# Gated attention on one core: weights and context turned by the host, centring on VectorE and GpSimd, scores in column halves, and a new order of work

## What is computed

```
ln_out = _ln(_layernorm(x), ln_w, ln_b)
q  = _ln(fp8_linear(ln_out, wq))      # 16 heads of 128, 2 heads in each of 8 groups
k  = _ln(fp8_linear(ln_out, wk))      # 8 groups of 128
v  = fp8_linear(ln_out, wv)
qx = _ln(fp8_linear(ln_out, wqx))
kx, vx = split(cond @ w_kv_x.T)       # cond is ctx_2048; kx is normalised too
core = softmax(q k / sqrt(128)) v     # inside each batch of 64 tokens
xout = softmax(qx kx / sqrt(128)) vx
catq = fp8(clip(concat(core, xout) / proj_smooth))
x = x + tanh(g_xattn[0]) * (catq @ wproj.T) * scale
```

## Time and profile before

| | us |
|---|---|
| median of 3 runs | 1088.43 (1088.19 to 1090.18) |
| the profiled execution | 1089.46 |
| its span, first to last instruction | 1087.70 |
| opening, to the first projection | 35.47 |
| steps 0 and 1 | 49.33 |
| steps 2 to 13 | 324.22 (27.02 each) |
| step 14 | 26.37 |
| step 15 and the tail, to the last matmul at L315 | 61.48 |
| all that follows | 590.83 |

### The profile page before, as it was taken

One profiled execution on the slowest core, in us unless ns is written; L12 is line 12 of the kernel. 1 busy time (PEld: TensorE's weight loads), 2 busy tenths in 40 slices (PEclk: granted clock), 3 DMA queues, 4 the chain that ended last, 5 costly groups with the idle time before them and its releaser, 6 DMA issues. The chain is left out here.

```text
span 1087.7 us, 19039 instructions
## 1 busy us (share of the span) xinstructions
PE 981.8 (90%) x6752; PEld 822.5 (76%) x6752; DVE 749.8 (69%) x1301; ACT 539.2 (50%) x1655; POOL 268.0 (25%) x416
## 2 busy tenths in 40 slices
PE   3689999999999999956899999995999999699998
PEld 3579999999999998855677777773666665577776
DVE  8858878777878787776544454445688888666653
ACT  5566666666666665622433333323455554233332
POOL 2133333333333333302422222202010111323130
PEclk8799999999999999976799999997899998799999
DMA  5001020101010100004111111001000000110001
GB/s 180 1 2 59 2 59 2 59 2 59 2 60 1 60 4 18 2 1 176 44 47 47 47 46 46 3 0 59 1 1 0 0 0 2 58 59 30 29 0 39
DMA packets 22823, 35.40 MB, mean 33 GB/s; under 512 B 2016, under 2 KB 19552, under 8 KB 21600
## 3 DMA queue, kind: packets, MB, share of 16 engines
q1 hardware_dynamic: 22464, 34.38, 9.6%
q10 hardware_dynamic: 288, 0.10, 0.0%
HBM read 33.42 MB, written 1.05 MB: 32 GB/s over the span
## 5 line engine op out<-in xcount | busy, mean ns | idle before, releaser
L251 PE MATMUL ps<-wt_hi,xq 128*128 128x256 f32 (+1 forms) x512 | 124.7, 278 | 13.0 <-issue 10.3
L251 PE MATMUL ps<-wt_lo,xq 128*128 128x256 f32 (+1 forms) x512 | 122.2, 281 | 0.0
L458 ACT ACTIVATE square<-ps 128x128 bf16<-128x128 f32 x384 | 100.6, 293 | 39.7 <-PE ps L251 39.6
L251 PEld LDWEIGHTS ps<-wt_hi,xq 128*128 128x128 f32 x512 | 98.4, 192 | 17.2 <-issue 15.3
L1624 ACT ACTIVATE ca_probs<-ps 128x512 f32<-128x512 f32 x128 | 69.5, 595 | 82.8 <-PE ps L1544 82.8
L251 PEld LDWEIGHTS ps<-wt_lo,xq 128*128 128x128 f32 x512 | 98.9, 193 | 0.0
L1684 DVE TENSOR_REDUCE context_mx<-ps 128x4 f32<-128x1024 f32 x64 | 76.9, 1201 | 26.4 <-PE ps L1516 26.4
L596 POOL TENSOR_TENSOR rstd<-rstd,half_neg 128x6 f32<-128x6 f32 x64 | 87.2, 1362 | 5.0
L1210 POOL TENSOR_TENSOR moe_w_lo<-moe_w_all,moe_w_hi 128x384 fp32r<-128x384 f32 x48 | 54.8, 1176 | 135.4 <-ACT moe_w_hi L1311 135.4
L458 ACT ACTIVATION_READ_ACCUMULATOR square<-ps 128x1 f32 x384 | 86.0, 225 | 0.0
L1375 DVE TENSOR_TENSOR moe_act_g<-moe_act_g,ps 128x512 f32<-128x512 f32 x48 | 33.0, 687 | 70.5 <-PE ps L1246 70.5
(11 more groups left out here) (225 smaller groups left out, 2685.8 us busy)
## 6 DMA issues: line engine op xcount, KB each, us to landing
moe_w_all<-in_experts SPq DMA_DIRECT2D x8, 1152.0 KB, 5.4
wp_rows<-in_wproj SPq DMA_DIRECT2D x16, 256.0 KB, 2.9
ffn_codes<-in_codes SPq DMA_DIRECT2D x8, 384.0 KB, 3.2
ffn_w_scales<-in_code_scales SPq DMA_DIRECT2D x8, 384.0 KB, 3.9
w_rows<-in_wq SPq DMA_DIRECT2D x8, 256.0 KB, 3.7
w_rows<-in_wqx SPq DMA_DIRECT2D x8, 256.0 KB, 3.9
w_rows<-in_w_kv_x SPq DMA_DIRECT2D x16, 128.0 KB, 3.6
x_rows<-in_x SPq DMA_DIRECT2D x2, 512.0 KB, 5.1
```

The lines of the kernel that those rows point to most:

```text
L251: last = mm(ps[:, first + bank, col:col + n], left[:, c, tokens], w[:, c, wcol:wcol + n], start=(j == 0), stop=(j == len(steps) - 1))
L458: last = nc.scalar.activation(square[:, j, :], ps[:, bank, (j % 4) * P:(j % 4) * P + P], ACT.Square, scale=float(HD) ** -0.5, accum_out=su ...
```

## The change

- The host hands the weights over turned and grouped (`in_wt`, one load of 1 MB a group), the output weights as well (`in_wp`), and the context turned (`in_ctxT`). All matmuls and transposes on weights and context are gone from PE's part, and `centre` with them.
- Centring: DVE sums each of the six blocks over its 128 columns (`sum_weights`, one reduction of 128 x 768 for each of two chunks), POOL divides the sum and subtracts it in place, with the input scale (`centre_weights`, seven `tensor_scalar` of 128 x 128 and a tiny one for a chunk). ACT copies a chunk as the high part (128 x 1024), DVE subtracts for the low part (128 x 1024). The output weights are one ACT copy and one DVE subtraction of 128 x 1024 a group.
- Each score matmul is cut in two, one a head: 64 stationary columns, 64 moving ones, and output partitions 0 to 63 or 64 to 127.
- `take` is on ACT for both attentions. The values have three buffers instead of two, the squares two instead of one.
- All 16 steps are written out, with two more for what is left over, and their order is new: PE projects two tiles, works on scores and values, projects two more, and a unit's softmax now reaches from step `h + 1` into step `h + 2`.
- The opening has two roundings of the inputs in place of three; the third and the fourth stand in DVE's step 0. Ahead of the first input scaling ACT now has the high parts of the first weights, which wait for POOL's centring.

Core of the diff:

```diff
-            for j in range(4):
-                turn_weights(0, j, 4 + j)
...
+            def centre_weights(g, c):
+                pool.wait_ge(s["wt_summed"], CH * g + c + 1)
+                nc.gpsimd.tensor_scalar(w_mean[:, c, :], w_mean[:, c, :], 1.0 / HD, None, ALU.mult).then_inc(s["wt_mean"], 1)
...
+                for blk, scale in enumerate((0, 0, 2, 2, 4, None, None, 6)):
...
+                        last = nc.gpsimd.tensor_scalar(cols, cols, mean, factor, ALU.subtract, ALU.mult)
...
+            def sum_weights(g, c):
...
+                nc.vector.tensor_reduce(w_mean[:, c, :], w_in[:, c, 0:CENTRED * P].rearrange("p (b d) -> p b d", b=CENTRED),
+                                        AX.X, ALU.add).then_inc(s["wt_summed"], 1)
...
+            def weights_low(g, c):
+
+                dve.wait_ge(s["wt_hi_done"], CH * g + c + 1)
+                nc.vector.tensor_tensor(wt_lo[:, g % 2, c, :], w_in[:, c, :], wt_hi[:, g % 2, c, :].bitcast(F32), ALU.subtract
+                                        ).then_inc(s["wt_lo_done"], 1)
...
-                    last = mm(ps[:, S_BANK, b * SEQ:b * SEQ + SEQ], qT[:, r, batch].rearrange("p h s -> p (h s)"),
-                              kT[:, r, batch * SEQ:batch * SEQ + SEQ], start=True, stop=True)
+                    for head in range(HPG):
+                        last = mm(ps[SEQ * head:SEQ * head + SEQ, S_BANK, b * SEQ:b * SEQ + SEQ], qT[:, r, batch, head, :],
+                                  kT[:, r, batch * SEQ:batch * SEQ + SEQ], start=True, stop=True)
...
+                if i == 0 and h < 2:
+
+                    pe.wait_ge(s["quantised"], CH * h + CH)
...
+            for c in range(CH):
+                nc.scalar.copy(ctx_hi[:, c, :], ctx_in[:, c, :]).then_inc(s["c_high"], 1)
+            for c in range(CH):
+                weights_high(0, c)
...
+                if h == 0:
+
+                    quantise_rows(2)
+                if ahead and h % 2 == 0:
+                    sum_weights(g + 1, 0)
+                if ahead and h % 2 == 0:
+                    sum_weights(g + 1, 1)
+                if is_unit(h - 2):
+                    quantise(h - 2, 1)
```

609 lines of the change are left out of this document (253 added, 356 removed).

## The result

The changed kernel takes **1097.49 us** (median of 4 runs, 1096.78 to 1097.61). The kernel before took 1088.31 beside it; the ratio is 1.007, with a 95% interval of 1.0051 to 1.0089. The forecast was 1061, with a range of 1044 to 1083. The sign was wrong.

| stage | before | forecast | after |
|---|---|---|---|
| opening, to the first projection | 35.47 | 40.1 | 47.45 |
| steps 0 and 1 | 49.33 | 58.3 | 63.29 |
| steps 2 to 14 | 350.59 | 311.4 | 331.37 |
| step 15 and the tail | 61.48 | 59.5 | 62.41 |
| all that follows | 590.83 | 590.8 | 590.98 |

What follows compares the result with a forecast made beforehand. PE was taken to bound steps 2 to 13 at 27.02 us each. Opening +4.7, steps 0 and 1 +9.0, steps 2 to 14 -39.2 and tail -2.0 summed to -27.5, giving 1061 us, range 1044 to 1083.

Steps and rivals of the forecast that it cites:

- I take 0.3: POOL's centring operation of 128 x 128: 0.3 us between bounds of 0.13 and 0.39, 2.4 a chunk.
- The rival built on this price: POOL's centring on the path at 1.0 us an operation: +32 us, 1093, chance 0.07.
- PE bounds it.: Kernel before, steps 2 to 13: PE busy 316.56 of 324.22 us, so PE bounds the step of 27.02.
- The new step, walked: Timeline from the second projection's end: tile 0 normalised at 1.9, an odd step 23.2 us long.
- A step with POOL never in the way: Better rival, POOL never delaying a tile: 22.9 us a step, 1047 in all, chance 0.17.
- The shared wait: Even steps, DVE and POOL blocking each other during centring: 1.3 us late, bounds 0 and 2.5, step 24.5.
- Opening +4.7: Before the first projection: sums, centring and copies ahead of input scaling, PE starting at 40.1; bounds 0 and +9.
- Steps 0 and 1 +9.0: Third and fourth roundings in DVE's step 0 make PE wait: 58.3 us instead of 49.33.
- Halves at 1.15: Each score cut in halves takes 1.15 us instead of 1.70, saving 1.1 a step.
- PE's loss of 2.2 and 1.1 a step: PE's work per step falls 2.2 us by dropped weight turning and 1.1 by halved scores, to 23.7.
- Tail, -2.0: Step 15 and the tail: 59.5 us instead of 61.48, last projection ending at 16.2.
- Scores at 3.4: Rival with score halves not overlapping, 3.4 us a score: a step of 27.3, 1104 in all, chance 0.03.

Runs made afterwards that it cites:

- e1: The changed kernel with POOL's seven centring operations a chunk left out, sums and waits kept: 1066.8 us.
- e4: The changed kernel with POOL subtracting broadcast means in two 128 x 384 operations a chunk, factors put into ACT's and DVE's copies: 1079.3 us.
- e3: The kernel before with only its scores cut in halves: 1089.7 us, ratio 1.001.
- e16: The changed kernel with ACT's high copy of output weights moved ahead of the keys of tiles 2 and 3 in odd steps: 1093.7 us.
- e12: The changed kernel with POOL's chunk 0 behind the roots of tiles 2 and 3 (even step), chunk 1 behind those of tiles 0 and 1 (odd): 1087.1 us.
- e5: The changed kernel with input scalings ahead of ACT's high weight copies, both roundings ahead of DVE's low copies, third rounding before step 0: 1086.2 us.
- e9: A price list, not a version: POOL's centring replaced by groups of four operations a chunk of one form each; no kernel time given.

## Why the prediction was wrong, step by step

- **"I take 0.3" for POOL's operation of 128 x 128.** This is the first term that failed, and the dearest. It measured 0.78 alone and 0.94 on average. The bounds were rows of other forms: a cast by the column, and a two-tensor operation by a third. The price list shows that neither the form nor the fixed part carries over. The rival built on this price ("at 1.0 us", 1093, chance 0.07) described what came: the opening at +14.5 (measured +12.0), steps 0 and 1 at +13.9 (+14.0), 2.9 behind tile 2 in an even step (2.4). e1 puts the whole centring at 30.7 us, and e4, with a chunk as cheap as forecast, has the forecast's opening and steps 0 and 1 to 0.1. That rival deserved far more, since no row bounded the operation from above.
- **"PE bounds it."** Wrong as far as e3 tells: 1.1 a step less for PE brought nothing. The check with step 14 had pointed that way (2.7 less work, 0.8 less time), and the prediction took it for a remark on the order instead of on the bound.
- **The new step, walked: "tile 0 is ready at 1.9".** It was 3.5 in the step shown. The take on ACT ended where the walk had it (190.36, 3.0 ahead of the end of the second projection). But the rounding took 4.1 for 3.3, and the root 2.34 for 1.36, as the two hold each other up. This is the second step that failed. The lock was known and was booked for the centring only, not for the pair that meets in every step; e16 prices it at 0.96 in an odd step. That tile 0 comes 0.6 later behind an odd step was walked and is right: moving the copy of the output weights took 0.57 off an even step's wait (e16). A step with POOL never in the way had been put at 22.9; in e1 it is 24.2, and 24.4 on average.
- **"The shared wait", +1.3 in even steps.** The sum of the even step, 24.5, was too small by 2.1: the queue behind POOL cost 2.4 where 1.3 was booked (e12), and the other 1.0 is the wait for tile 0. Where the centring is in nobody's way in the queue, the lock costs 0.5 (e12, odd steps).
- **Opening +4.7**: +12.0. The mechanism was right (two chunks ahead of the scaling), its price was that of POOL. **Steps 0 and 1 +9.0**: +14.0, with the rounding in step 0 behind tile 3, as walked; the fourth rounding ended at 83.7, and step 1 started at 83.80 instead of 73.9. Another place for the roundings (e5) or for POOL's chunks (e12) takes 4.6 or 4.9 of it away.
- **Halves at 1.15**: right, 1.08. Their gain of 1.1 a step was not: with what PE waits for, 0.03 to 0.32 in the changed kernel and 0.54 without the centring. **PE's loss of 2.2 and 1.1 a step**: right; step 14 has 24.22 less a wait of 1.82, 22.4 of PE's work.
- **Tail, -2.0**: +0.9. The last projection of step 15 ended 17.1 behind its start instead of 16.2, by the same wait for tile 0, and the rest took 45.3 instead of 43.3.
- **Loads free, the rest untouched** (590.98 for 590.83): right.
- **The working itself** has slips. The mean of 24.5 and 23.2 is 23.85, not 23.95, and step 14 centres nothing and counts as an odd one: 309.4 for the thirteen steps instead of 311.4, so the terms missed by 2 more than the sum shows. The reduction of 768 columns is 1.02 by its own row, not 0.9; it measured 0.88. Scores at 3.4 would make PE's sum 28.2, not 27.0, a rival that did not come.

The span is 35.3 us over the forecast: 7.3 in the opening and 5.0 in steps 0 and 1, which are POOL's price (e1 gives 9.8 and 8.0 back there), 20.0 in steps 2 to 14, 2.9 in the tail and 0.1 behind it. Of the 20.0, six even steps lost 2.4 each to the queue where 1.3 had been counted, about 7. The remaining 13, 1.0 a step, are put down to the wait for tile 0, as what is left. The lower clock in steps 2 and 10 has almost no part in it: they took 27.1 and 28.1 instead of 26.6, but the odd steps behind them 23.7 and 23.6 instead of 24.55, so these pairs took 50.83 and 51.72 for 51.15.

So about 19 of the 35 are POOL's price with the queue behind it, and 13 the wait for tile 0. Neither turned the sign alone: with the first miss only, the span would have been about 8 below the kernel before, and with the second only, about 14 below.

## What to carry to other kernels

Before a price goes into a sum, look for a row of the same engine, the same operation and the same kinds of operands; if there is none, the chance must go to the far side of the bound, and on GpSimd one wide operation with a broadcast tensor comes before many narrow ones with scalars per partition. A full engine is no proof of the bound: take some of its work away where it stands now, and see whether the step gets shorter. When work moves to an engine that another one queues on or locks, walk each pair of instructions that meet, in every step, not only the new ones.

## What the runs showed of the hardware

- GpSimd, 128 partitions, fp32 (e9, the last figure from e4): `tensor_scalar` with two scalars per partition 0.58, 0.81 and 1.23 us for 64, 128 and 256 columns; with one 0.96, with one constant 0.89, with two constants 0.41 for 256; `tensor_tensor` with a broadcast second tensor 0.40, 0.61 and 0.83 for 128, 256 and 384.
- Two fp32 matmuls of 64 x 64 on two halves of the columns go side by side: 32 records in 1.08 us (changed kernel) against 16 of double width in 1.70 (kernel before).
- A GpSimd root of 128 x 6 takes 1.32 to 1.35 us alone and 2.34 beside the last operation of a VectorE rounding; a `tensor_scalar` of 0.60 took 3.44 beside two VectorE operations (e5).
- Waits of PE can cost more than their length. Behind 1.17 and 0.69 in step 2 the granted clock went from 1.00 to 0.50 for some 3 us; in e16 the same happened in each even step, at about 1.5 us a time. But the same two waits left it at 1.00 in steps 4, 6, 8 and 12 of the changed kernel, and in step 4 of e12 it fell behind a single wait of 1.82. The kernel before, whose PE waited 0.3 at most in steps 2 to 13, stayed at full clock there, and so did its version with halves (e3), with 36 waits of up to 0.7.
